# A quantised product and a two-step gated layer on one core: two tiles' last two column blocks computed as seven block products

## The reference

```
q1 = fake_quant(layernorm(x));  q2 = fake_quant(ctx)     # round(v / s + z) clipped to 0..255, minus z, times s
x  = x + tanh(g1) * (q1 @ q2)
W  = (U * S) @ V.T                                       # rank 512
x  = x + tanh(g2) * (layernorm(x) @ W.T)
```

## Time and profile before

| | us |
|---|---|
| median of 3 runs | 588.17 (587.01 to 588.31) |
| profiled execution, time | 587.26 |
| profiled execution, span | 585.4 |
| TensorE busy | 568.0 |
| VectorE busy | 445.0 |
| ScalarE busy | 236.3 |
| GpSimd busy | 194.6 |

### The profile page before, as it was taken

How to read it: one execution, slowest core, us unless ns; L and a number is a source line. 1 busy time by engine, 2 the same in 40 slices (tenths; PEclk the granted TensorE clock), 3 DMA queues, 4 the chain that set the end, 5 groups by cost and what they waited for, 6 DMA issues and landing times.

```text
span 585.4 us, 7495 instructions
## 1 busy us (share of the span) xinstructions
PE 568.0 (97%) x2688; PEld 259.2 (44%) x2688; DVE 445.0 (76%) x796; ACT 236.3 (40%) x269; POOL 194.6 (33%) x146
## 2 busy tenths in 40 slices
PE   1899999999999999999999999999999999999998
PEld 0344444444444444444444444444444444444444
DVE  6878889996178973779978799788597986888222
ACT  4899978822122413648723612102530135003200
POOL 2999750000305127847541720210044005310000
PEclk9999999999999999999999999999999999999999
DMA  8999995638927797789965262423854087403722
GB/s 274 387 387 386 342 275 125 125 112 173 273 73 199 182 239 189 219 231 382 277 158 154 60 138 54 125 73 69 220 108 143 2 179 163 125 1 70 165 55 108
DMA packets 145940, 102.73 MB, mean 175 GB/s; under 512 B 108784, under 2 KB 109040, under 8 KB 145904
## 3 DMA queue, kind: packets, MB, share of 16 engines
q1 hardware_dynamic: 136912, 84.96, 54.9%
q10 hardware_dynamic: 8992, 17.30, 9.0%
HBM read 58.99 MB, written 16.78 MB: 129 GB/s over the span
## 4 chain that ended last, share of the span: by engine, by line
PE 93%; DVE 3%; ACT 1%; POOL 1%; DMA 1%; issue 1%; ACTq 0%; DVEq 0%
PE bank L616 23%; PE bank L692 19%; PE bank L661 11%; PE bank L697 9%; PE bank L755 9%; PE bank L760 9%; PE bank L756 9%; PE bank L579 2%; DMA ring<-in_x_dram 1%; DVE qn L1234 1%; DVE ring L1333 1%; POOL q L279 1%; ACT qn L884 1%; DVE st L1203 0%; PE bank L711 0%
## 5 line engine op out<-in xcount | busy, mean ns | idle before, releaser
L285 POOL TENSOR_SCALAR ring<-ring,bvec 128x2048 f32<-128x2048 f32 x16 | 33.5, 2094 | 260.3 <-DVE bvec L1246 260.3
L616 PE MATMUL bank<-q,qT 128*128 128x512 f16 x512 | 117.6, 381 | 0.0
L692 PE MATMUL bank<-v_hl,xT 128*128 128x512 f16 x448 | 101.3, 379 | 0.0
L290 POOL TENSOR_TENSOR ring<-ring,corr 128x512 f32<-128x512 f32 x64 | 87.1, 1392 | 23.1 <-ACT corr L966 22.1
L755 PE MATMUL bank<-u_hl,hbuf 128*128 128x512 f16 x208 | 78.9, 379 | 0.0
L756 PE MATMUL bank<-u_hl,hbuf 128*128 128x512 f16 x208 | 78.8, 379 | 0.0
L279 POOL TENSOR_SCALAR q<-u8r,const 128x1024 f16<-128x1024 uint8 x52 | 67.2, 1304 | 32.2 <-ACT u8r L863 29.6
L616 PEld LDWEIGHTS bank<-q,qT 128*128 128x128 f16 x512 | 50.3, 98 | 61.1 <-issue 0.8
L692 PEld LDWEIGHTS bank<-v_hl,xT 128*128 128x128 f16 x448 | 43.8, 98 | 52.1
L914 ACT ACTIVATE ln<-ln,const 128x1 f32<-128x1 f32 x16 | 4.7, 293 | 143.6 <-DVE ln L1343 143.6
L1417 DVE SCALAR_TENSOR_TENSOR ring<-bank,cy,ring 128x512 f32<-128x512 f32 x63 | 46.2, 744 | 16.9 <-PE bank L760 16.9
(11 more groups left out here) (174 smaller groups left out, 780.5 us busy)
## 6 DMA issues: line engine op xcount, KB each, us to landing
out_dram<-ring SPq DMA_DIRECT2D x63, 256.0 KB, 3.4
ring<-in_x_dram SPq DMA_DIRECT2D x62, 256.0 KB, 4.3
v_hl<-in_ctx_dram SPq DMA_DIRECT2D x26, 512.0 KB, 11.5
stage<-in_ctx_dram ACTq DMA_DIRECT2D x17, 512.0 KB, 5.9
u_hl<-in_L_ffn_V_dram SPq DMA_DIRECT2D x8, 512.0 KB, 11.5
corr<-in_ctx_dram ACTq DMA_DIRECT2D x8, 512.0 KB, 6.4
stage<-in_ctx_dram SPq DMA_DIRECT2D x6, 512.0 KB, 11.4
q<-in_ctx_dram ACTq DMA_DIRECT2D x4, 512.0 KB, 10.1
```

The costliest lines, as they stand in the source:

```text
L290: nc.gpsimd.tensor_tensor(xq(t, n), xq(t, n), corr[:, n * W:(n + 1) * W], ALU.add).then_inc(x1_pre, 1)
L616: mm = nc.tensor.matmul(unit_bank(t, n)[:, :], qT_of(t)[:, k, :], q2[:, n, k, :], start=(k == 0), stop=(k == KT - 1))
L692: nc.tensor.matmul(h_bank(u)[:, :], x_home(u, g)[:, half, k % 8, :], v_hl[:, k, 0, :], start=(g == 0 and a == 0 and half == 0), stop=False)
```

## The change

Column blocks 2 and 3 of tiles 4 and 5 are computed together as seven products of 8 matmuls (`early_quad`), between `mm4(2)` and tile 5's first two blocks. Blocks 0 and 1 of both tiles stay as they were. The sums T1 to T4 are made by VectorE into rooms that are free then: `xs` (T1), `stage` (T2), `u8r` (T3) and `xT` (T4); S1 to S4 into `xn` and `qn`. The products use banks 0 to 2. The quantisation to bytes of tiles 4 to 7 moves from VectorE to ScalarE. The steps of VectorE, ScalarE and the SyncE queue around it are put in a new order: tile 5's loads stand ahead of its transpose, the hidden transpose of tile 3 and the transpose of tile 6 at other places, the context's first refills and conversions behind the products P6 and P7. Further lines replace `unit` by `s_unit` in counts of blocks, as `s1_done` and `x1_ready` no longer count the four blocks.

```diff
+        EARLY = (TB // 2, TB // 2 + 1)
+        s_unit = lambda t, n: unit(t, n) if t < EARLY[0] else NQ * EARLY[0] + 2 * (t - EARLY[0]) + n if t in EARLY else \
+            unit(t, n) - NQ
...
-        Q_ACT = range(TB, NT)
+        Q_ACT = range(R, NT)
...
+        e_t1, e_t4 = t4_room, t1_room
+        e_t2, e_t3 = t2_room
+        e_seq = {k: i + 1 for i, k in enumerate((P1, P6, P2, P5, P7, P3, P4))}
+        e_bank = lambda k: bank[{P2: 0, P5: 1, P3: 1}.get(k, 2)]
...
+                elif t - 2 in EARLY:
+                    sp.wait_ge(e_done, NP)
...
+                    if u == EARLY[0]:
+                        sp.wait_ge(e_done, P4 + 1)
...
+            store(1, 0)
+            store(1, 1)
+            h_transpose(2)
+            store(1, 2)
+            store(1, 3)
             q_transpose(4)
-            turn(1)
+            for n in range(NQ):
+                load_x(5, n)
             q_transpose(5)
-            turn(2)
+            turn(2, False)
+            h_transpose(3)
             x_transpose(4)
+            q_transpose(6)
             for n in range(NQ):
                 store(3, n)
-            q_transpose(6)
...
+                        if t == EARLY[1]:
+                            pe.wait_ge(e_read, e_seq[(P2, P3)[n]])
+                        if t == EARLY[1] + 1 and n == 0:
+                            pe.wait_ge(e_read, NP)
...
+            def early_product(k):
+                a, b = EARLY
+                left, right = {P1: (a_part(a, 0), b_part(2, 0)), P5: (s_part(0), t_part(e_t1)),
+                               P6: (s_part(1), t_part(e_t2)), P3: (s_part(2), b_part(3, 1)),
+                               P7: (s_part(3), t_part(e_t3)), P2: (a_part(a, 1), b_part(2, 1)),
+                               P4: (a_part(b, 1), t_part(e_t4))}[k]
+                if k == P1:
+                    pe.wait_ge(x1_ready, s_unit(a, 1) + 1)
+                elif k == P6:
+                    pe.wait_ge(qT_in, 16 * (b - G + 1))
+                    pe.wait_ge(e_s_made, 2)
+                    pe.wait_ge(e_t2_made, 2)
+                    pe.wait_ge(e_read, e_seq[P1])
+                elif k == P5:
+                    pe.wait_ge(e_t1_made, 2)
+                elif k == P7:
+                    pe.wait_ge(e_s_made, 4)
+                    pe.wait_ge(e_t3_made, 2)
+                    pe.wait_ge(e_read, e_seq[P6])
+                elif k == P3:
+                    pe.wait_ge(e_read, e_seq[P5])
+                elif k == P4:
+                    pe.wait_ge(e_t4_made, 2)
+                    pe.wait_ge(e_read, e_seq[P7])
+                for i in range(KH):
+                    mm = nc.tensor.matmul(e_bank(k)[:, :], left[:, i, :], right[:, i, :],
+                                          start=(i == 0 and k in (P1, P2, P5)), stop=(i == KH - 1),
+                                          skip_group_check=k in (P6, P7, P4, P3))
+                mm.then_inc(e_done, 1)
...
-            s1(4)
+            s1_part(4, 0)
+            s1_part(4, 1)
             mm4(2)
-            s1(5)
+            early_quad()
+            s1_part(5, 0)
+            s1_part(5, 1)
...
+                if t == R:
+                    act.wait_ge(split_lo, VP + RT)
+                if t == EARLY[1] + 1:
+                    act.wait_ge(e_done, P7 + 1)
...
+            quantise(4)
             op2(4)
-            act.wait_ge(split_lo, VP + RT * NQ)
+            hid_hi(3)
+            root1(5)
+            quantise(5)
+            op2(5)
+            act.wait_ge(e_t4_made, 2)
+            act.wait_ge(e_done, P6 + 1)
             refill(CB)
             refill(CB + 1)
+            act.wait_ge(e_done, P7 + 1)
             stream(0, 2)
-            root1(5)
-            op2(5)
             root2(4)
             x_hi(4)
             stream(2, 4)
-            hid_hi(3)
+            root1(6)
+            quantise(6)
+            op2(6)
             root2(5)
-            root1(6)
-            x_hi_half(5, 0)
-            op2(6)
-            x_hi_half(5, 1)
+            x_hi(5)
+            hid_hi(4)
             stream(4, 6)
-            hid_hi(4)
             root1(7)
+            quantise(7)
...
+            def early_t3():
+                for c in range(2):
+                    b12, b22 = [k_piece(flat2(b_part(3, h)), c, 2 * HW) for h in range(2)]
+                    tt(k_piece(e_t3, c, 2 * HW), b22, b12, ALU.subtract).then_inc(e_t3_made, 1)
+
+            def early_t2():
+                for c in range(2):
+                    dve.wait_ge(e_t3_made, c + 1)
+                    tt(k_piece(e_t2, c, 2 * HW), k_piece(e_t3, c, 2 * HW), k_piece(flat2(b_part(2, 0)), c, 2 * HW),
+                       ALU.add).then_inc(e_t2_made, 1)
+
+            def early_t1():
+                for g in range(2):
+                    dve.wait_ge(xT_in[g], 16 * x_dma(EARLY[0] - 1))
+                for c in range(2):
+                    b11, b12 = [k_piece(flat2(b_part(n, 0)), c, 2 * HW) for n in (2, 3)]
+                    tt(k_piece(e_t1, c, 2 * HW), b12, b11, ALU.subtract).then_inc(e_t1_made, 1)
+
+            def early_t4():
+                dve.wait_ge(mm3_half, 2 * EARLY[0])
+                for c in range(2):
+                    dve.wait_ge(e_t2_made, c + 1)
+                    tt(k_piece(e_t4, c, 2 * HW), k_piece(flat2(b_part(2, 1)), c, 2 * HW), k_piece(e_t2, c, 2 * HW),
+                       ALU.subtract).then_inc(e_t4_made, 1)
+
+            def early_s_sums():
+                a, b = EARLY
+                A11, A12, A21, A22 = [flat2(a_part(t, h)) for t in EARLY for h in range(2)]
+                S1, S2, S4, S3 = s_room
+                dve.wait_ge(qT_in, 16 * (b - G + 1))
+                dve.wait_ge(xs_lo, 2 * a)
+                tt(S1, A21, A22, ALU.add).then_inc(e_s_made, 1)
+                dve.wait_ge(e_s_made, 1)
+                tt(S2, S1, A11, ALU.subtract).then_inc(e_s_made, 1)
+
+            def early_s_sums_34():
+                a, b = EARLY
+                A11, A12, A21, A22 = [flat2(a_part(t, h)) for t in EARLY for h in range(2)]
+                S1, S2, S4, S3 = s_room
+                tt(S3, A11, A21, ALU.subtract).then_inc(e_s_made, 1)
+                dve.wait_ge(e_s_made, 2)
+                tt(S4, A12, S2, ALU.subtract).then_inc(e_s_made, 1)
+
+            def early_add(k):
+                a, b = EARLY
+                t, n = {P1: (a, 2), P5: (b, 3), P6: (a, 3), P3: (a, 3), P7: (b, 3), P2: (a, 2), P4: (b, 2)}[k]
+                if k in (P3, P7, P2):
+                    dve.wait_ge(e_read, e_seq[{P3: P6, P7: P5, P2: P1}[k]])
+                else:
+                    dve.wait_ge(x1_pre, unit(t, n) + 1)
+                dve.wait_ge(e_done, k + 1)
+                stt(xq(t, n), e_bank(k)[:, :], C_A, xq(t, n), ALU.mult, ALU.add).then_inc(e_read, 1)
+                if k in (P3, P7, P2, P4):
+                    dve.wait_ge(e_read, e_seq[k])
+                    nc.vector.bn_stats(st2[:, t % R, n, :], xq(t, n)).then_inc(st2_ready, 1)
...
             variance1(4)
+            y_unit(1, 1)
             quantise(4)
-            y_unit(1, 1)
             y_unit(1, 2)
+            early_t3()
+            y_unit(1, 3)
             row_correction(4)
-            y_unit(1, 3)
-            x1_unit(4, 0)
+            early_t2()
+            early_t1()
+            hid_lo(3)
             sums1(5)
             variance1(5)
+            quantise(5)
+            x1_unit(4, 0)
             x1_unit(4, 1)
-            quantise(5)
+            early_t4()
             y_unit(2, 0)
-            x1_units(4, (2, 3))
+            row_correction(5)
+            y_unit(2, 1)
+            early_s_sums()
+            y_unit(2, 2)
+            y_unit(2, 3)
+            early_add(P1)
+            early_s_sums_34()
+            early_add(P6)
+            early_add(P2)
+            early_add(P5)
+            early_add(P7)
+            early_add(P3)
             stats2(4)
-            row_correction(5)
+            early_add(P4)
             x_lo_half(4, 0)
-            y_unit(2, 1)
-            x_lo_half(4, 1)
-            y_unit(2, 2)
-            hid_lo(3)
-            y_unit(2, 3)
-            x1_units(5, range(NQ))
-            variance2(5)
+            x1_unit(5, 0)
             sums1(6)
             variance1(6)
-            scale2(5)
+            x1_unit(5, 1)
+            quantise(6)
             y_unit(3, 0)
-            quantise(6)
+            x_lo_half(4, 1)
+            stats2(5)
             y_unit(3, 1)
+            row_correction(6)
+            x_lo_half(5, 0)
             y_unit(3, 2)
             y_unit(3, 3)
-            row_correction(6)
-            x_lo(5)
-            hid_lo(4)
+            x_lo_half(5, 1)
             sums1(7)
             variance1(7)
             quantise(7)
+            hid_lo(4)
             x1_units(6, (0, 1))
```

More of the change, by code:

```diff
@@ L150, in gated_block_program @@
         p_done = sem("p_done")
+        e_t3_made = sem("e_t3_made")
+        e_t2_made = sem("e_t2_made")
+        e_t1_made = sem("e_t1_made")
```

(28 more changed lines are left out.)

## The result

The changed kernel takes 592.94 us (median of 6, 591.18 to 595.69) against 587.07 us (median of 6, 586.86 to 588.31): ratio 1.0088, 95% interval 1.0069 to 1.0106. I had forecast 587.0 in a range of 586.0 to 589.9. Ratios and intervals in this document are those on record, which leave out executions in a slower state (three of the nine in experiment 1); they are not quotients of the medians, which would be 1.0100 here. The profiled execution has a span of 590.9 us, 5.5 more than before.

A forecast was written before the change was run, and what follows sets the result against it. TensorE was taken to bound the kernel, busy 568.0 of 585.4 us. Off the median of 588.17, -1.73 for matmuls + 0.2 + 0.3 for stalls = -1.2 us gave 587.0 us, range 586.0 to 589.9.

The forecast's parts named there:

- Steps 1 to 5: Tiles 4 and 5 through the seven products: eight matmuls fewer, 1.73 us less; added VectorE and ScalarE work costs 0.2.
- the 0.2 us for P6: Stall allowed where P6 wants the bank from which P1 is still being read: 0 to 0.5 us, taken as 0.2.
- The first term: Matmuls of tiles 4 and 5: 120 instead of 128, eight fewer at 0.2158 us, 1.73 us less.
- Step 6: After P4: tile 4's root at 182.5, output row (3,0) at 195.1 in time, tile 3's stores some 4 us later.
- Step 8: Tile 5's transpose into xT behind tile 7's loads: issued 209.9, 6.7 us, landed 216.6 when needed; cost nothing.
- step 7: Tile 7's x loads, called decisive: landing in 3.6 us, qT issued at 220.3, landed 227.2; cost 0.3 us.
- Rival D: TensorE's granted clock falls in a stall, so the change frees less than it says; no chance of its own.
- bound 8: Upper bound for landing of tile 5's transpose into xT: 220.6, where it was needed at 216.6.
- rival B: Tile 7's x loads take 6.3 to 8.7 us as before, delaying its first block: 589.7 to 592.1; chance 0.17.
- Step 9: Behind tile 7's first block nothing new waits, so what is gained at 228 stays to the end; free.

The follow-up runs named there:

- experiment 1: Changed kernel with ScalarE taking tile 4's second root and high halves before the context conversions: 591.56 us, ratio 1.0034 to the kernel before.
- experiments 10 and 11: Changed kernel with tile 4's root first and refills later: with eight unused matmuls added 587.99 us (ratio 1.0004), without them 586.55 us (0.9981).
- experiment 5: Changed kernel with 16 more matmuls, results unused, ahead of tile 5's hidden product: 595.52 us, ratio 1.0136 to the kernel before.
- Experiment 3: Changed kernel with context conversions 4 and 5 and their two refills moved behind tile 7's quantisation: 589.00 us, ratio 1.0028 to the kernel before.
- experiment 4: Changed kernel with VectorE's two T4 sums each computed twice, same values: 594.30 us, ratio 1.0114 to the kernel before.

## Why the prediction was wrong

*Steps 1 to 5 held.* The products ran without a gap; T1 was done at 153.2 (I took 155; T2's two sums, 2.35 us, were not slowed, and GpSimd's step beside them took 3.85 us instead of 2.0; T1's two took 5.12), output row (2,0) at 163.7 (166.0), P1 read at 172.1 (172.5 to 173.7), so that the 0.2 us for P6 was not needed. The first term is 1.73, and experiments 10 and 11 give 1.4 of it.

*Step 6 failed by one size that I never bounded:* "the root for tile 4 (182.5)" took for the first chunks the landing of the kernel before, 4.0 us (issued at 142.5, converted from 146.54 on the earlier trace rows), where SyncE had issued nothing for 2 us.

```profile
142.50 0.91 ACTq L870 DMA_DIRECT2D stage<-in_ctx_dram  x2
```

They were issued at 174.8 beside two x loads and a hidden transpose and took 7.2 and 8.2 us (6.2 to 9.4 in the other changed versions, 10.6 once in experiment 5). The root came at 185.5. Of this, output row (3,0) was late: "195.1 (needed 196.6)" became 197.6, a wait of 1.4.

*Step 8 failed in size and in its price:* I took 6.7 us from 209.9, "nothing"; it was 10.3 from 211.4. Of my two rows the one of 6.7 us, tile 3's, had no refill beside it, as the first was issued at 142.5. The one of 9.8 us is this same transpose, with two refills issued 3.4 and 1.7 us ahead of it. In the new order two come 1.2 and 2.9 us behind it, and I had noted them "at 211.4" in step 7, as good news for the x loads; so rows 18 was the nearest row, and 209.9 + 9.8 would have given 3.1 us of wait. The upper bound that I wrote there, 220.6, is 4.0 us of wait and near the truth, but no rival carried it. Experiment 3 shows what the refills cost the transpose: 5.8 us without them.

*The clock had no term.* Rival D got no chance because a wait of 0.4 us shows no fall; the four waits of 3.5 to 4.5 us do, and behind 4.1 us it cost 1.7 us on top. The range should have had bound 8 with the clock behind it: 1.4 + 4.1 + 1.7 - 1.7 is 5.5, past its upper end of 2.8 over the median of before.

*Step 7 and rival B* had the right place in the queue and the wrong member: the x loads landed in 3.3 to 4.3 us, as the arbitration rule of the Trainium skill (DMA: Bandwidth & Descriptors, "Queues, rings and completion order") suggested; by the same rule the transpose, with ScalarE's two refills in turn with it, had to pay, and the trace agrees with that (10.3 against 5.8 us). I applied it to one of two transfers. The rest of step 7 did not hold: tile 7's qT was issued at 222.8 (I had 220.3) and took 10.1 us (6.9), and landed 5.7 us later than I had it. The wait on xT covered that, as step 8 had said of such losses; so it is luck that nothing shows at tile 7's block. *Step 9 held:* no new wait behind 230 us in the changed kernel.

## What to carry to other kernels

When a transfer is moved out of one place, look for whoever stands in its new one, and price that transfer with the landing of the busiest comparable case. A step that gates another engine's chain belongs ahead of work that waits for a DMA. A TensorE wait can cost more than itself: those of 3.5 to 4.5 us did here.

## What the runs showed of the hardware

- A 512 KB transpose of SyncE's queue landed 4.2 to 4.4 us after its issue with no load beside it, in 5.3 to 6.6 behind four x loads of its own queue where no refill was issued in the 4 us behind it, in 7.8 to 10.7 behind these and beside two 512 KB refills of ScalarE's queue, and in 13.4 at worst.
- Tile 7's qT, a transpose of the same size, landed in 4.2 to 4.3 us where the refills waited for it (three runs), in 6.4 to 7.4 where the first refill came 1.1 us behind it (seven, the kernel before among them), and in 10.1 to 11.0 where one came 0.9 us or less behind it or ahead (changed kernel, experiments 1 and 4). In these three a hidden transpose was also issued 1.3 us ahead of it, in the others 3.6 us and more; which of the two does it was not separated.
- TensorE's granted clock fell behind idle stretches of 3.5 to 4.5 us and not behind 1.9 to 2.9 us. What that cost on top is not in the order of the waits: 2.9 us behind 3.5 (28 matmuls in 8.98 us, experiment 5), 1.6 behind 3.8 (16 in 5.25 instead of 3.62), 1.7 behind 4.1 (5.28), 2.75 behind 4.5 (6.37, experiment 4).
- Where TensorE waited for landings the times were wider: before 586.9 to 588.3, changed kernel 591.2 to 595.7, experiment 1 586.7 to 603.5.
